# Four-layer graph kernel on one core: half-step queries in the second attention layer, the first layer's weighting behind its sums, marks for four steps at once

## The reference

```python
h = jnp.maximum(_layernorm(x, axis=-1), 0.0)
x = x + _L0_gnn_ref(h, ...)      # 16 heads of 8; softmax over the edges of a source node
h = ...; x = x + _L1_gnn_ref(h, ...)   # 8 heads of 32; softmax over the edges of a target node
h = ...; x = x + _L2_gnn_ref(h, ...)   # sums by relation, batch norm
h = ...; x = x + _L3_gnn_ref(h, ...)   # 4 heads of 64; softmax over target nodes

# L1, per edge e:
scores = einsum('ehd,ehd->eh', q[dst], k[src] + ep[:, None, :]) * scale * ew[:, None]
m = segment_max(scores, dst); ex = exp(scores - m[dst]); s = segment_sum(ex, dst)
out = segment_sum((ex / s[dst])[:, :, None] * v[src], dst)
```

## Time and profile before

| | us |
|---|---|
| median of 3 runs | 7706.99 (7702.69 to 7715.14) |
| profiled execution, own time | 7714.56 |
| its span in the profile | 7712.8 |
| busy PE, DVE, ACT, POOL | 5533.7, 4805.5, 3687.5, 5209.9 |

### The profile page before, as it was taken

One profiled execution on the slowest core, in us unless ns is written; L12 is line 12 of the kernel. 1 busy time (PEld: TensorE's weight loads), 2 busy tenths in 40 slices (PEclk: granted clock), 3 DMA queues, 4 the chain that ended last, 5 costly groups with the idle time before them and its releaser, 6 DMA issues. The chain is left out here.

```text
span 7712.8 us, 119806 instructions
## 1 busy us (share of the span) xinstructions
PE 5533.7 (72%) x30906; PEld 4182.6 (54%) x30906; DVE 4805.5 (62%) x14770; ACT 3687.5 (48%) x11072; POOL 5209.9 (68%) x5181
## 2 busy tenths in 40 slices
PE   6777675555559898967888888797555555767774
PEld 5666665555546666644666666564443444545553
DVE  8666666666658788877999999311222224555555
ACT  1333333222247777754888888332000003777773
POOL 4777777777777777743777776212777773777773
PEclk9777787777789999988999999898777777888786
DMA  4333341111145665645777776313444444444443
GB/s 146 78 80 79 79 110 34 36 36 34 36 110 155 159 157 155 157 120 145 202 200 200 202 202 172 110 58 92 109 109 108 109 108 73 109 110 110 109 110 88
DMA packets 1041601, 885.39 MB, mean 115 GB/s; under 512 B 749049, under 2 KB 857617, under 8 KB 1040823
## 3 DMA queue, kind: packets, MB, share of 16 engines
q0 software_dynamic: 259600, 658.46, 31.6%
q1 hardware_dynamic: 726977, 162.08, 11.1%
q10 hardware_dynamic: 54374, 57.20, 2.2%
HBM read 736.38 MB, written 140.99 MB: 114 GB/s over the span
## 5 line engine op out<-in xcount | busy, mean ns | idle before, releaser
L1302 POOL DMA_INDIRECT edges_kv<-kv,edges_rec x1712 | 1867.5, 1091 | 569.2 <-issue 473.2
L1449 PE MATMUL banks<-edges_kv,edges_hot 128*128 128x288 f32 (+2 forms) x5136 | 1482.4, 437 | 310.4 <-DVE edges_kv L1777 232.5
L1449 PEld LDWEIGHTS banks<-edges_kv,edges_hot 128*128 128x128 f32 x5136 | 1024.4, 210 | 577.7 <-issue 324.7
L1968 POOL DMA_INDIRECT edges_rows<-rel,edges_rec x856 | 809.4, 946 | 382.1 <-issue 257.1
L574 POOL DMA_INDIRECT by_src_records<-sort_by_src_rec,sort_by_src_pos_i x808 | 798.4, 988 | 326.6 <-issue 225.1
L1302 POOL DMA_INDIRECT edges_kv<-feat,edges_rec x856 | 828.5, 968 | 268.6 <-issue 242.8
L1984 PE MATMUL banks<-edges_rows,edges_hot 128*128 128x256 f32 x1712 | 630.3, 533 | 462.5 <-DMA edges_rows<-rel,edges_rec 423.3
L574 POOL DMA_INDIRECT by_dst_records<-sort_by_dst_rec,sort_by_dst_pos_i x808 | 787.5, 975 | 246.4 <-issue 241.5
L661 DVE SCALAR_TENSOR_TENSOR sort_junk<-banks,sort_hot_lo 128x128 bf16<-128x128 f32 x1616 | 437.7, 287 | 659.7 <-PE banks L723 646.6
L1984 PEld LDWEIGHTS banks<-edges_rows,edges_hot 128*128 128x128 f32 x1712 | 434.2, 266 | 658.8 <-DMA edges_rows<-rel,edges_rec 263.8
L1604 ACT ACTIVATE edges_off<-columns,edges_column 128x128 bf16<-128x128 f32 x2568 | 785.7, 393 | 0.0
(11 more groups left out here) (456 smaller groups left out, 11919.1 us busy)
## 6 DMA issues: line engine op xcount, KB each, us to landing
edges_kv<-kv,edges_rec POOLq DMA_INDIRECT x1712
sort_feat<-in_edge_attr_dram SPq DMA_DIRECT2D x100, 256.0 KB
rel<-tables_stage SPq DMA_DIRECT2D x100, 252.0 KB
by_dst_records<-by_dst_blank ACTq DMA_DIRECT2D x21, 800.0 KB
edges_rec<-by_dst_records SPq DMA_DIRECT2D x26, 592.0 KB, 7.6
by_src_records<-by_src_blank ACTq DMA_DIRECT2D x1, 13696.0 KB, 52.1
edges_rows<-rel,edges_rec POOLq DMA_INDIRECT x856, 2.7
edges_kv<-feat,edges_rec POOLq DMA_INDIRECT x856
```

Source lines behind the costliest of these rows:

```text
L1302: pool.indirect_dma_start(kv[:, r, c, 0:koff + DIM], None, tab, bass.IndirectOffsetOnAxis(ap=reci[:, b, c, idx:idx + 1], axis=0)).then_inc ...
L1449: last = pe.matmul(ps[:, 6 + m % 2, 0:OW], hot[:, b % 2, c, :], kv[:, b % BUFS, c, koff:koff + OW], start=(c % 2 == 0), stop=(kind != 1 an ...
L1968: pool.indirect_dma_start(rows[:, r, c, :], None, tab, bass.IndirectOffsetOnAxis(ap=reci[:, b, c, idx:idx + 1], axis=0)).then_inc(gathered ...
```

## The change

Three things.

In the second layer, PE uses the first layer's order: `expand_half` spreads four tiles' queries at once into two banks (1 and 2, or 4 and 5), and DVE multiplies a half-step by one instruction of 1024 columns where there were two of 512. The matrix of segment borders leaves `front` and is made by `turn_seg` in a corner of bank 6, as in the first layer; ACT reads it in `penalties` after `part(*ahead, 1)`, and `sums` waits for that before pair 2 writes to the bank.

In all attention layers, `tie` and `place` work on four steps at once (32 columns) in each fourth step.

In the first layer, the sums of a half-step (`add_sums` 0 and 1, or 2 and 3) stand ahead of `weigh`; before, one stood behind it, one behind the scans or behind the reduction.

```diff
-    BANKS = (1, 2, 5)
-    HALF_BANKS = (1, 3)
+    HALF_BANKS = {0: (1, 3), 1: (1, 4)}.get(kind)
@@ expand_half
+                    if kind == 1:
+                        pe.wait_ge(hot_t_ready, n(2, h + 1))
+                        for i in range(2):
+                            rows = [part[:].bitcast(F32R)[:, bass.ds(blocks[2 * h + i], 1), :].rearrange("p o w -> p (o w)") for part in q]
+                            for c in range(2):
+                                for part in range(2):
+                                    last = pe.matmul(ps[:, first + i, QW * c:QW * c + QW], hot_t[:, b % 2, 4 * h + 2 * i + c, :], rows[part],
+                                                     start=(part == 0), stop=(part == 1), skip_group_check=True)
+                        last.then_inc(at_edges, 1)
+                        return
@@ sums, on PE
-                        if kind == 0 and m == 2 and newest:
+                        if kind < 3 and m == 2 and newest:
                             pe.wait_ge(front_copied, n(1, 1) + 3)
@@ body of the second layer, on PE
                     if gone:
                         with_past(*gone, 3)
                     if inside:
-                        expand(j, b, (2,))
+                        expand_half(j, b, 1)
                     if oldest:
                         sums(*oldest, 0)
-                        if kind == 1:
-                            with_past(*oldest, 0)
-                    if inside:
-                        expand(j, b, (3,))
-                    if oldest and kind == 1:
-                        with_past(*oldest, 1)
+                        with_past(*oldest, 0)
                     if ahead:
                         spread_lo(*ahead, 1)
+                    if oldest:
+                        with_past(*oldest, 1)
                     if older:
                         turn_back(*older)
                     if ahead:
-                        expand(*ahead, (0,))
+                        turn_seg(*ahead)
+                        expand_half(*ahead, 0)
                     if oldest:
                         sums(*oldest, 1)
-                        if kind == 1:
-                            with_past(*oldest, 2)
-                    if ahead:
-                        expand(*ahead, (1,))
+                        with_past(*oldest, 2)
@@ tie, on DVE
-                    dve.tensor_tensor(tied[:], rec[:, b, :, seg], O.cont_all[:, bass.ds(n(G, 0), G)], ALU.is_equal).then_inc(placed, 1)
+                    dve.tensor_tensor(tied[:, 0:some, :], rec[:, b:b + some, :, seg],
+                                      O.cont_all[:, bass.ds(n(G, 0), some * G)].rearrange("p (s c) -> p s c", c=G), ALU.is_equal
+                                      ).then_inc(placed, 1)
@@ multiply_half, on DVE
-                    for m in (2 * h, 2 * h + 1):
-                        k2 = kv[:, r, 2 * m:2 * m + 2, 0:QW]
-                        dve.wait_ge(at_edges, n(PAIRS, m + 1))
-                        dve.tensor_tensor(k2, bank_of(b, m), k2, ALU.mult).then_inc(edges_used, 1)
+                    k4 = kv[:, r, 4 * h:4 * h + 4, 0:QW]
+                    dve.wait_ge(at_edges, n(2, h + 1))
+                    dve.tensor_tensor(k4, half_of(h), k4, ALU.mult).then_inc(edges_used, 1)
@@ body, on DVE
+                    if gone and kind == 0:
+                        add_sums(*gone, blocks, 0)
+                        add_sums(*gone, blocks, 1)
                     if oldest:
                         weigh(*oldest, 0)
...
-                    if gone and kind == 0:
-                        add_sums(*gone, blocks, 1)
...
+                    if gone and kind == 0:
+                        add_sums(*gone, blocks, 2)
+                        add_sums(*gone, blocks, 3)
                     if oldest:
                         weigh(*oldest, 1)
```

More of the change, by code:

```diff
@@ L1115, in edge_layer @@
     QW = L.q_width
-    DU = {0: 2, 1: PAIRS, 3: 1}[kind]
+    DU = {0: 2, 1: 2, 3: 1}[kind]
     HOT = (F32, F32R, None, BF16)[kind]
-    BANKS = (1, 2, 5)
-    HALF_BANKS = (1, 3)
+    HALF_BANKS = {0: (1, 3), 1: (1, 4)}.get(kind)
     LO_BANKS = {0: (5, 5), 1: (3, 3), 3: (3, 2)}[kind]
-    SEG_BANK = {1: 0, 3: 5}.get(kind)
-    SCORE_AT = (0, 2 * P) if kind == 0 else (4, P)
+    SEG_BANK = {3: 5}.get(kind)
+    SCORE_AT = {0: (0, 2 * P), 1: (0, P), 3: (4, P)}[kind]
     EXP_AT = 3 * P if kind == 0 else 2 * P
@@ L1375, in expand_half, with expand @@
                     last.then_inc(at_edges, 1)
-                def expand(j, b, pairs):
+                def expand(j, b):
                     n = at(j, b)
                     blocks = blocks_of(pe, O, j, b, UNROLL)
[L1381 to L1400, removed]
+                    pe.wait_ge(hot_t_ready, n(2, 2))
+                    pe.wait_ge(edges_used, n(1, 0))
+                    for c in range(G):
+                        last = pe.matmul(ps[:, 1, 3 * H * c:3 * H * c + 3 * H], hot_t[:, b % 2, c, :],
+                                         q_parts[:, bass.ds(blocks[c // 2], 1)].rearrange("p o i h -> p (o i h)"), start=True, stop=True)
+                    last.then_inc(at_edges, 1)
                 def turn_scores(j, b):
@@ L1421, in turn_back @@
                     pe.wait_ge(max_kept, n(1, 1))
-                    ahead = after(j, b, 2)
-                    if ahead and kind == 1:
-                        pe.wait_ge(front_copied, at(*ahead)(1, 1))
                     if not first_steps(j, b, 1):
@@ L1538, in body_by_heads @@
                     if ahead:
-                        expand(*ahead, None)
+                        expand(*ahead)
                     if beyond:
@@ L1601, in one_hot @@
                     n = at(j, b)
-                    act.wait_ge(placed, n(2, 2))
+                    batch = j * (UNROLL // LOAD) + b // LOAD
+                    act.wait_ge(placed, 2 * batch + 2)
                     for c in range(G):
-                        last = act.activation(off[:, c, :], C.columns[:, c % 2, :], ACT.Abs, bias=column[:, b % 2, c:c + 1], scale=-1.0)
+                        last = act.activation(off[:, c, :], C.columns[:, c % 2, :], ACT.Abs, bias=column[:, batch % 2, b % LOAD, c:c + 1],
+                                              scale=-1.0)
                     last.then_inc(off_ready, 1)
@@ L1682, in body @@
                         part(*ahead, 1)
-                        if kind == 0:
-                            penalties(*ahead)
+                        penalties(*ahead)
                         hot_rows(*ahead, 1)
@@ L1852, in body @@
                         gone = None
-                    here = (j, b) if inside else None
+                    here = (j, b) if inside and b % LOAD == 0 else None
                     last_add = (lambda: add_sums(*gone, blocks, 3)) if gone else None
@@ L1864, in body @@
                         multiply_half(j, b, 0)
+                    if gone and kind == 0:
+                        add_sums(*gone, blocks, 0)
+                        add_sums(*gone, blocks, 1)
                     if oldest:
                         weigh(*oldest, 0)
-                    if gone:
-                        add_sums(*gone, blocks, 1 if kind > 0 else 0)
+                    if gone and kind > 0:
+                        add_sums(*gone, blocks, 1)
                     if older:
                         scan(*older, here)
-                    elif inside:
+                    elif here:
                         tie(j, b)
                         place(j, b)
-                    if gone and kind == 0:
-                        add_sums(*gone, blocks, 1)
                     if inside:
@@ L1881, in body @@
                         multiply_half(j, b, 1)
+                    if gone and kind == 0:
+                        add_sums(*gone, blocks, 2)
+                        add_sums(*gone, blocks, 3)
                     if oldest:
                         weigh(*oldest, 1)
-                    if gone and kind == 0:
-                        add_sums(*gone, blocks, 2)
                     if inside:
-                        finish_scores(j, b, last_add)
-                    elif gone:
+                        finish_scores(j, b, last_add if kind > 0 else None)
+                    elif gone and kind > 0:
                         last_add()
```

44 lines of the change are left out of this document (23 added, 21 removed).

## The result

| | before | after |
|---|---|---|
| median, us | 7710.74 (7702.69 to 7715.14, 4 runs) | 7753.78 (7751.6 to 7762.84, 4 runs) |
| ratio | | 1.0058, 95% interval 1.0046 to 1.007 |
| span of the profiled execution | 7712.8 | 7749.9 |
| busy PE, DVE, ACT, POOL | 5533.7, 4805.5, 3687.5, 5209.9 | 5538.8, 4790.5, 3688.7, 5249.5 |

The changed kernel is slower by 43 us (0.46% to 0.70%). The forecast was 18 us slower, in a range of 7665 to 7775. DVE has 15 us less to do and POOL 40 us more, with the same 5181 instructions: its gathers last longer in the second layer.

A forecast was written before the change was run, and what follows sets the result against it. The prediction took PE with ACT to bound the second layer, and a loop through POOL and its gathers' landing the first. 7707 + 50 (second layer) − 32 (first layer) = 7725 us, marks at 0; range 7665 to 7775.

The forecast's parts named there:

- the main case: Whole kernel: the forecast of 7725 us, with its own range of 7700 to 7745 and a chance of 0.40.
- The second layer's term: Second layer, PE: pair 3's spread now stands ahead of the sums; 0.47 us a step, 50 us lost, ends 27 and 62.
- the first layer's: First layer, DVE: sums ahead of the weighting shorten the holds of gathers; 32 us gained, ends 0 and 58.
- the loop: Second layer: PE's pasts and ACT's copies wait for each other and set the pace, 11.36 us a step.
- Its low end: Second layer's PE order: 0.25 us a step comes back from between the two pasts, leaving 27 us lost.
- DVE's saving: Second layer: one multiplication of 1024 columns saves 0.39 us a step, hidden, taken as 0, appearing as wait for the scores.
- penalties cost nothing: Second layer, ACT: penalties made later are covered by the eight `off` instructions, so costed at nothing.
- the rival in which it is the pace: Second layer: DVE is the pace, so 42 and 32 us are gained, 7633 us; chance 0.18.
- half the price: Rival in the second layer: only 27 us lost, with 32 gained, 7702 us; chance 0.22.
- the working of the half-step: First layer: a gather loses 0.25 us instead of 0.52, a gain of 0.27 a half-step, at most 58 us.
- the rival in which the reorder gives nothing: First layer: something else holds the gather, or the sums wait for ACT's copy; 7757 us, chance 0.12.
- the rival of 7945: First layer: the hold passes from second sum to weighting, 0.88 us more a half-step, 188 us; chance 0.08.

The follow-up runs named there:

- e1: The changed kernel with the first layer's DVE order and the marks as before: 7762.47 us beside 7708.75 for the kernel before, ratio 1.0075.
- f1: The changed kernel; in the second layer POOL gathers seven tiles of eight, SP fills the eighth with fixed rows: 7746.19 us beside 7707.3, ratio 1.0057.
- f2: The kernel before; in the second layer POOL is relieved of the eighth tile, filled by SP with fixed rows: 7702.2 us beside 7707.3, ratio 0.9992.
- f4: h1 with POOL relieved of one gather in eight in the second layer, filled by SP with fixed rows: 7711.65 us in a single run.
- g2: g1 with pair 2's spread ahead of the past of pair 3 in the second layer: 7711.37 us beside 7716.52 for the kernel before, ratio 1.0.
- g1: The kernel before with the first layer's new order and the marks for four steps, without the second layer's half-steps: 7723.25 us beside 7716.52, ratio 1.0012.
- e2: The kernel before with only the first layer's sums moved ahead of the weighting: 7705.43 us beside 7708.75, ratio 0.9995.
- e5: The changed kernel; in the first layer a half-step's first sum stands between key and product, the second between product and weighting: 7797.15 us, ratio 1.0122.
- f5: e5 with POOL relieved of one gather in eight in the first layer, filled by SP with fixed rows: 7681.51 us in a single run.
- e4: The changed kernel with PE spreading pair 3 between the pasts of pairs 0 and 1, as before; DVE's single product kept: 7795.28 us, ratio 1.0111.
- h1: The changed kernel with the second half's spread moved ahead of the past of pair 3 on PE: 7745.88 us, ratio 1.0043.

## Why the forecast held, and where its size was off

The measured 7753.8 lies in the range of 7665 to 7775, but 29 us above the sum, and 9 above the 7745 at which the main case ended. The second layer's term was right, the first layer's was mis-sized.

The second layer's price was 50 us, and e1 measures 54. Its mechanism is the one named: the spread ahead of the sums grew by 0.46 us, and the relieved pair f1 and f2 puts 11.76 against 11.33, 0.43 a step, 46 us. f4, with the spread off the loop, adds to this: 11.21. That 0.47 met 0.46 so closely has luck in it: the prediction calls 0.39 to 0.58 the time of two multiplications, where a pair's spread is four, and picked a value between. (Its low end, 0.47 − 0.25, is 24 us and not 27; nothing hangs on that.) The rest, some 0.1 a step, is what the forecast did not have: 1.8 holds a step by the key addition instead of one, and with them 51 waits of DVE for a landing. DVE's saving was hidden, as said, and penalties cost nothing. Its free time shows as these waits for landings and not, as forecast, as a wait for the scores.

One row was misread: in the earlier trace rows the 188 us of 193 in the second layer are DVE's, and ACT had 165. So DVE was nearly full, with 0.3 us to spare in a step, and the rival in which it is the pace deserved a closer look than "there are gaps around its work" gave it. It falls all the same: in the same stretch after the change DVE is busy for 173 of 193 us, and the step is longer. That of half the price falls with e1. So small a margin also fits how little g2 gained by taking 0.58 off the loop: 11.39 a step in g1's profile, 11.27 in g2's.

The term that was mis-sized is the first layer's: 32 us gained, with 0 and 58 as ends. The profiles show 6 to 11 with order and marks; the timed runs show 3 for the order alone (−3 to 11, e2), and none with the marks (g1). The step that failed is the working of the half-step: I let the second sum begin at s + 1.82, the weighting at about s + 2.2 and the gather still at s + 1.90, with the next one due only when the weighting is over. The second sum waits for the first one's write, so it begins at s + 2.15 (2709.40 − 2707.25) and the weighting at s + 2.53, in the half-step ahead of the one shown:

```profile
2707.25 0.69 DVE L1789 TENSOR_TENSOR edges_kv<-banks,edges_kv 128x512 f32<-128x512 f32 x1 [0.72 <-DMA edges_kv<-kv,edges_rec]
...
2709.18 0.95 POOL L1301 DMA_INDIRECT edges_kv<-kv,edges_rec  x1 [0.30 <-issue]
...
2709.40 0.46 DVE L1760 TENSOR_TENSOR acc<-edges_pair_sums,acc 128x288 f32 x1 [0.36 <-ACT edges_pair_sums L1636]
...
2709.78 1.22 DVE L1771 TENSOR_TENSOR edges_kv<-edges_kv 128x1024 f32<-128x1024 f32 x1
...
2710.43 1.38 POOL L1301 DMA_INDIRECT edges_kv<-kv,edges_rec  x1 [0.30 <-issue]
```

The profile puts this one wait down to ACT's copy, but its length is that of the others. The gather at s + 1.93 is free, as hoped, and the next one, at s + 3.18 and not s + 3.4, meets the weighting. Nor do the gathers keep their place: one began at s + 1.9 to 2.0 in 122 of 189 half-steps before, and in 29 of 191 after. Over the stretch from 2300 to 3350, the weighting held 173 gathers by 0.51 us each before, and the sums 17 by 0.25. After, the weighting held 106 by 0.60, and the sums 84 by 0.18. That saves 0.08 us on a half-step, where I had 0.27, and the mean gather falls to 1057 ns instead of about 1040. The wait between the sums stood in the code and had no row before, as other work lay between them. It isn't itself the loss, as e5 showed, which has no such wait and longer holds. That the layer's time follows the holds in the changed kernel too is argued from e5 and f5, not tested. So the nearest of the rivals in time is the one in which the reorder gives nothing, 7757, and I gave it 0.12.

The Trainium skill's page "SBUF — State Buffer", section "Who interferes with whom", infers that a plain tensor_tensor doesn't hold up the making of descriptors, which led to that same 7757. The time agrees and the reason doesn't: in the rows a gather begun 0.02 us behind the start of a plain tensor_tensor lasts 2.01 us instead of 0.95, in e5, where such holds are longer by 0.44 us a step, the kernel is 43 us slower, and by f5 and the sum there 112 us of e5's first layer hang on them.

That the hold passes on from the second sum to the weighting, the rival of 7945, is refuted by the layer's mean of 1057 ns: passing on would have given each half-step 1.40 of hold, and a mean of 1300. It does happen, but rarely: of 93 gathers begun during a second sum with the weighting right behind it, 85 got in between and 7 were held to the end of the weighting, and eight gathers of just over 2 us stand in the layer, none before.

What stays open is why the first layer's profile gains 11 us with order and marks together and the median doesn't, and what puts the key addition just ahead of a gather nearly twice a step in the new order. The sums without their chain weren't tried, since two pairs can write to one block.

## What to carry to other kernels

Where two loops between engines have the same length in a profile, relieve one of them and look whether the step moves: the relief of POOL parted them in four kernels, where reordering alone gave misleading answers twice (e4, h1). Ahead of a move, put every instruction that it lengthens on the loop, and read in the code which waits come up when two links of a chain become neighbours. An engine that holds another by running beside it sets a price for each place in the order, and a move that looks free changes that price.

## What the runs showed of the hardware that I had not expected

In both layers eight gathers at 1.25 us and their holds add up to the step, within 0.2 us, in quick and slow orders alike: 11.3, 11.8 and 12.2 us in the second layer (before, after, e4). In the relieved kernels the mean gather changed freely (1031 ns in f1, 1140 in f2, 990 in f4) without the step following it (11.76, 11.33, 11.21). So the sum says only that POOL is never idle, not that it leads.
